# A two-layer graph network on one core: VectorE's maxima, shift, normalization and ELU results at other places of its order

## What is computed

```python
def _gat_layer(x, src, dst, W, a_src, a_dst, bias, concat):
    h = (x @ W).reshape(N, H, C)
    al_s, al_d = einsum('nhc,hc->nh', h, a_src), einsum('nhc,hc->nh', h, a_dst)
    e = leaky_relu(al_s[src] + al_d[dst], 0.2)
    m = segment_max(e, dst)
    ex = exp(e - m[dst])
    alpha = ex / (segment_sum(ex, dst)[dst] + 1e-16)
    out = segment_sum(h[src] * alpha[:, :, None], dst)   # concat or mean over heads, + bias

h = maximum(layernorm(x), 0)
x = x + gat_layer(elu(gat_layer(h, ..., 4 heads)), ..., 1 head)   # with self-loops
h = maximum(layernorm(x), 0)
x = x + gcn(relu(gcn(h)))       # D^-1/2 (A + I) D^-1/2 h W + b, twice
```

## Time and profile before

| what | value |
|---|---|
| median of 3 runs | 1179.64 us (1179.39 to 1180.54) |
| the profiled execution | 1182.3 us |
| its span | 1180.2 us |
| TensorE busy | 1115.9 us, 95% |
| VectorE busy | 839.0 us, 71% |
| ScalarE busy | 513.9 us, 44% |
| mean granted TensorE clock | 0.984 of full speed |
| first layer's rounds | about 245 to 750 us |
| second attention layer | about 780 to 905 us |

### The profile page before, as it was taken

One profiled execution on the slowest core, in us unless ns is written; L12 is line 12 of the kernel. 1 busy time (PEld: TensorE's weight loads), 2 busy tenths in 40 slices (PEclk: granted clock), 3 DMA queues, 4 the chain that ended last, 5 costly groups with the idle time before them and its releaser, 6 DMA issues. The chain is left out here.

```text
span 1180.2 us, 17595 instructions
## 1 busy us (share of the span) xinstructions
PE 1115.9 (95%) x7126; PEld 1045.3 (89%) x7126; DVE 839.0 (71%) x1394; ACT 513.9 (44%) x1052; POOL 54.3 (5%) x50
## 2 busy tenths in 40 slices
PE   5999999999999999999999999858999899999998
PEld 5878886789989998999999999758999899899998
DVE  7998896889768887789668778879757633341163
ACT  4232322376447654556547644335536612431110
POOL 4200001020000000000000000520000000000000
PEclk9999999989999999999999999968999999999999
DMA  6133130021011100201020100022002200000321
GB/s 230 68 103 117 41 122 18 1 63 54 1 42 49 54 1 1 90 22 34 1 68 23 54 1 1 10 91 72 27 27 103 83 1 1 27 14 1 131 77 55
DMA packets 27618, 58.44 MB, mean 50 GB/s; under 512 B 3492, under 2 KB 6152, under 8 KB 27536
## 3 DMA queue, kind: packets, MB, share of 16 engines
q1 hardware_dynamic: 27344, 56.96, 14.5%
q10 hardware_dynamic: 192, 0.32, 0.1%
HBM read 41.73 MB, written 15.54 MB: 49 GB/s over the span
## 5 line engine op out<-in xcount | busy, mean ns | idle before, releaser
L1456 PE MATMUL banks<-hs,ring_hi 128*128 128x258 f32 (+1 forms) x1600 | 299.8, 288 | 6.8 <-DVE z L1051 6.8
L1456 PEld LDWEIGHTS banks<-hs,ring_hi 128*128 128x128 f32 (+1 forms) x1600 | 249.0, 188 | 8.7 <-DVE z L1051 8.0
L1456 PE MATMUL banks<-hs,ring_lo 128*128 128x258 f32 (+1 forms) x800 | 227.1, 284 | 0.0
L247 ACT ACTIVATE e<-banks,al 128x256 f32<-128x256 f32 (+1 forms) x500 | 194.6, 493 | 38.0 <-PE banks L232 38.0
L1456 PEld LDWEIGHTS banks<-hs,ring_lo 128*128 128x128 f32 (+1 forms) x800 | 150.8, 189 | 0.0
L255 ACT ACTIVATE ring_hi<-pf 128x512 fp32r<-128x512 f32 (+1 forms) x125 | 81.6, 652 | 134.7 <-DVE pf L266 130.1
L1486 PE MATMUL banks<-w_hi,oT_hi 128*128 128x384 f32 (+1 forms) x320 | 109.5, 342 | 5.9 <-DVE shiftT L1130 4.5
L1486 PE MATMUL banks<-w_lo,oT_hi 128*128 128x384 f32 (+1 forms) x320 | 108.3, 338 | 0.0
L1486 PE MATMUL banks<-w_hi,oT_lo 128*128 128x384 f32 (+1 forms) x320 | 108.2, 338 | 0.0
L264 DVE TENSOR_TENSOR e<-e 128x512 f32<-128x512 f32 (+1 forms) x125 | 84.5, 676 | 33.2 <-ACT e L247 32.7
L1330 PE MATMUL banks<-w_hi,xT_hi 128*128 128x512 f32 x240 | 96.7, 403 | 1.2 <-DVE xT_lo L827 0.6
(11 more groups left out here) (265 smaller groups left out, 2106.2 us busy)
## 6 DMA issues: line engine op xcount, KB each, us to landing
h_scratch<-stage SPq DMA_DIRECT2D x30, 256.0 KB, 2.0
hs<-h_scratch SPq DMA_DIRECT2D x30, 256.0 KB, 2.9
w_st<-in_L_gnn_W SPq DMA_DIRECT2D x4, 1536.0 KB, 7.4
w_st<-in_L_gnn_W SPq DMA_DIRECT2D x16, 384.0 KB, 3.4
gw_st<-in_L_gnn_W SPq DMA_DIRECT2D x12, 384.0 KB, 4.2
xr<-in_x SPq DMA_DIRECT2D x9, 384.0 KB, 10.1
rows<-in_x SPq DMA_DIRECT2D x9, 384.0 KB, 5.8
x_scratch<-rows SPq DMA_DIRECT2D x9, 384.0 KB
```

The source lines that it names most:

```text
L247: last = nc.scalar.activation(self.e[:, local % 2, a, i, 0:n], self.p_shift[:, a, 0:n], ACT.Exp, bias=scores[a][:, g * G + i:g * G + i + 1])
L1456: last = nc.tensor.matmul(p_a[0:m, dt, half, 0:HH], wt.ring[a][:, s // G, s % G, dt * P:dt * P + m], hs[:, s, b, half * HH:(half + 1) * HH ...
```

## The change

No instruction is added or removed; instructions of VectorE and a few of TensorE stand at other places. With the diff's own order:

- In rounds c = 0 of heads 1 to 3, `normalize` of the last round and the first `add_products` block stand ahead of group 3's weights instead of behind them and group 2's low part.
- In rounds c = 4 of heads 0 to 2, `take_peaks(h, 0)` stands right behind the weights of group 0 and `take_peaks(h, 1)` right behind those of group 1 (they stood behind the low parts in groups 1 and 2). On TensorE the last two transposes of the maximum stand behind step 4 instead of 7, and the turned shift behind step 7 instead of 9. `keep_shift` stays in group 3.
- In every round `elu_out` stands ahead of group 4's weights (and in rounds c = 1 ahead of the split of weight parts 0 and 1), instead of between the low parts of groups 3 and 4.
- In the second layer the shift is turned behind step 4 and spread behind step 5 of chunk 0 (5 and 6 before), and in chunk 1 both `finish` calls stand behind group 2 instead of behind group 3.

```diff
--- before.py
+++ after.py
@@ -1135,7 +1135,12 @@
                     q = h * NC + c
                     last, second_last = before(q, 1), before(q, 2)
                     for g in range(NG - 1):
+                        if g == NG - 2 and c == 0 and h >= 1:
+                            normalize(last)
+                            add_products(second_last, range(1))
                         wt.weigh(nc, dve, counts, q, c, g)
+                        if c == NC - 1 and not final and g <= 1:
+                            take_peaks(h, g)
                         if second_last is not None and g == 0:
                             elu_lo(second_last, 0)
                         if q == 0 and g == 0:
@@ -1154,14 +1159,17 @@
                             nc.vector.tensor_copy(deg[:, :], p_d).then_inc(deg_done, 1)
                         if c == 0 and 1 <= g <= 2:
                             split_rows(h, g - 1)
-                        if c == NC - 1 and not final and g >= 1:
-                            (lambda: take_peaks(h, 0), lambda: take_peaks(h, 1), lambda: keep_shift(h))[g - 1]()
+                        if c == NC - 1 and not final and g == NG - 2:
+                            keep_shift(h)
                     scoring = final and c >= 2
                     row = (c - 2) * NDT
-                    if last is not None:
-                        normalize(last)
-                    if second_last is not None:
-                        add_products(second_last, range(2))
+                    if c == 0 and h >= 1:
+                        add_products(second_last, range(1, 2))
+                    else:
+                        if last is not None:
+                            normalize(last)
+                        if second_last is not None:
+                            add_products(second_last, range(2))
                     if c == 0:
                         split_rows(h, 2)
                     if not final:
@@ -1178,12 +1186,12 @@
                         add_products(second_last, range(3, NB))
                     if c == 0:
                         split_rows(h, 3)
+                    if last is not None:
+                        elu_out(last)
                     if c == 1:
                         split_weights(h, range(2))
                     wt.weigh(nc, dve, counts, q, c, NG - 1)
                     wt.lo(nc, dve, q, c, NG - 2)
-                    if last is not None:
-                        elu_out(last)
                     wt.lo(nc, dve, q, c, NG - 1)
                     if c == 0:
                         split_rows(h, NG - 1)
@@ -1420,12 +1428,12 @@
                     for t in range(8):
                         last = nc.tensor.transpose(p_g[t // 4][:, t % 4 * P:(t % 4 + 1) * P], top[:, t * P:(t + 1) * P], ident[:, :])
                     last.then_inc(top_t, 1)
-                if s == 7:
+                if s == 4:
                     pe.wait_ge(reduced, 3 * h + 3)
                     for t in range(8, T):
                         last = nc.tensor.transpose(p_g[0][:, (t - 8) * P:(t - 7) * P], top[:, t * P:(t + 1) * P], ident[:, :])
                     last.then_inc(top_t, 1)
-                if s == 9:
+                if s == 7:
                     turn_shift(h + 1, p_g[1][0:4 * T, 0:P])
 
             def turn_out(q, dt):
@@ -1518,7 +1526,7 @@
                 pe.wait_ge(shift_out, HEADS + 2)
                 wt.broadcast(nc, pe, pick, shiftT[:, 2, :], SECOND + 1, 1)
 
-            half.tensor(pe, {1: turn_rest, 5: lambda: turn_shift(HEADS + 1, p_shift_rest), 6: spread_rest})
+            half.tensor(pe, {1: turn_rest, 4: lambda: turn_shift(HEADS + 1, p_shift_rest), 5: spread_rest})
 
 
 BANDS = [(0, 3 * P), (3 * P, 3 * P), (6 * P, N - 6 * P)]
@@ -1847,12 +1855,14 @@
         dve.wait_ge(b_in, 16)
         residual(0)
         for c in range(1, NC):
+            ends = NG - 3 if c == 1 else NG - 2
             for g in range(NG - 1):
                 wt.weigh(nc, dve, counts, SECOND + c, c, g)
                 if g >= 1:
                     wt.lo(nc, dve, SECOND + c, c, g - 1)
-            for t in range((c - 1) * NDT, c * NDT):
-                finish(t)
+                if g == ends:
+                    for t in range((c - 1) * NDT, c * NDT):
+                        finish(t)
             wt.weigh(nc, dve, counts, SECOND + c, c, NG - 1)
             wt.lo(nc, dve, SECOND + c, c, NG - 2)
             wt.lo(nc, dve, SECOND + c, c, NG - 1)
```

## The result

The changed kernel takes **1172.36 us** (median of 7 runs, 1171.01 to 1175.7) where the kernel before took 1179.64 beside it on the same chip; the ratio is 0.9945, 95% interval 0.9926 to 0.9964. It is faster by about 7 us. The forecast was 1168.3 in a range of 1164.5 to 1173.3: the direction and the range held, the time near the range's upper end, and the gain of 11.3 us was too high by some 4. The profiled execution took 1172.36 us as well; its span is 1170.3, 9.9 less than the 1180.2 of the earlier trace rows. One execution of the experiment with the second layer's part alone took 1514.74 us at a mean granted clock of 0.677 and is left out of its ratio.

The account below looks back on a forecast made before the run. TensorE is busy nearly all of 1180.2 us, so only its waits or clock move the time. Terms -5.4 - 4.05 - 4.8 + 1.1 + 0.4 + 1.5 = -11.3 from 1179.64 give 1168.3 us, range 1164.5 to 1173.3.

Parts of the forecast that it names:

- The maxima and the shift: Round 4 of heads 0 to 2: maxima wait goes, 0.83 of the copy's wait stays; gain 1.81 us a head, 5.4 in three.
- The normalization: Rounds 5, 10 and 15: TensorE's wait for it goes; gain 1.35 us a head, 4.05 in three.
- The ELU results, rounds 6, 11 and 16: First transpose's gain goes into the second's wait for the turned low part; 0.14 us lost in each, 0.4 in all.
- The ELU results, round 1: Early results push weight parts and their load, so the turned low part delays the second transpose: 1.1 us lost.
- The clock behind the round-1 wait: TensorE's clock falls behind the new 2.3 us wait in round 1: 1.5 us lost, bounds 0 and 2.8.
- The second layer's rows: Second layer, first tile's rows: TensorE resumes at 810.45 instead of 812.44, 0.7 of wait left; gain 2.0 us.
- The clock behind the second layer's rows: With the wait there shortened, TensorE's clock stays up behind it: 2.8 us more gain.
- The carry-over to the median: Profiled execution, 2.7 us above the median of the runs: the forecast gain of 11.3 was taken off the median, 1179.64.
- Those at 1171.1 and 1173.1 us: Rivals, second layer: only 2.0 gained as the clock falls behind another wait, or nothing as sums hold the rows; chance 0.13.
- the one at 1171.3: Rival: the clock falls also behind the 1.7 us waits of rounds 6 and 11, 2 x 1.5 us more; chance 0.15.
- The rival in which the change is slower: Weight-load chain longer in every head: 1.1 + 2.8 = 3.9 us a head lost, +1.3 to +5.7 (1185.3 us); chance 0.03.

Follow-up runs that it names:

- the second trace: The changed kernel run again unchanged, for a second look at its waits and clock: 1173.78 us, ratio 0.9932 to the kernel before.

## Why the prediction was right, and where it was off

- **The maxima and the shift** (1.81 a head): right in mechanism, the term was too large. It measured 1.50, and the wait left is 1.06, not 0.83. The step that failed is "the exponentials of group 3 ... nothing ahead of them is moved": TensorE's own transposes of the maxima are, and they push the second transpose by 0.25.
- **The normalization** (1.35 a head): right. No wait at rounds 5, 10 and 15. That the early ELU results save this gain, with 0.3 us of slack, was right as well; without them the wait is 1.80.
- **The ELU results, rounds 6, 11 and 16** (0.14 lost in each): the waits were right, 1.99 and 1.72 where 1.7 was forecast, the loss was not. The two full pieces came within 0.01 and 0.22 of the forecast because two errors cancel: with 1.50 for the maxima and 1.35 for the normalization they would be 2.85 shorter, and they are 3.03 and 3.24 shorter, so the early results gained 0.2 and 0.4 in rounds 6 and 11. With the ELU results alone the same pieces are 130.75 and 130.57 us, 0.1 and 0.2 under those before. In round 16 they lost 0.5 in the first trace, with a wait of 0.80 that I had not forecast, and nothing in the second, where that wait did not come; ScalarE's wait for the load of part 3 there was 0.79 and 0.24.
- **The ELU results, round 1** (1.1 lost): the mechanism was right, the term too small: 1.7 lost (1.9 in the second trace). I followed the push of the load of part 2 alone. Counted from the start of round 1's sums, ScalarE's copy of part 2 starts 1.21 and 1.07 later in the two traces, as forecast, but that of part 3 starts 1.69 and 1.93 later (9.99 us before, 11.68 and 11.92 now), and that is the whole loss. ScalarE waits for the load of part 3 0.86 and 1.24 us where it waited 0.38:

```profile
270.81 0.85 ACT L672 ACTIVATE w_hi<-w_st 128x768 fp32r<-128x768 f32 x1 [0.38 <-DMA w_st<-in_L_gnn_W]
```

  VectorE's push is 1.13 of that; why the load of part 3 comes another 0.6 and 0.8 later is open. And the wait of 2.3 that I gave was worked out with the clock low ahead of it; with the clock at 1.00 there it is 4.65, with the clock low 3.36.
- **The clock behind the round-1 wait** (1.5): it fell, for about 6 us and not 3. In the changed kernel 59.39 - (58.31 - 1.50) = 2.6 us; in the second trace 59.27, 2.5 us.
- **The second layer's rows** (2.0): right. The wait is 0.89 (0.7 expected). The piece got shorter by 2.9, of which 2.0 is the wait; the rest goes with the clock behind the wait of 3.97 at its start, which was low for less long in that execution (0.50, 0.50, 0.52 and 1.00 over the four stretches of 2 us behind it, where before it was 0.50, 0.50, 0.50 and 0.54). That 0.9 is luck and no gain of the change.
- **The clock behind the second layer's rows** (2.8): from one profiled execution to the other it came out, at 2.69. (I counted 36 matmuls in the 6.50 us where the earlier trace rows shows 38; with 38 the term is 3.0.) But I read 0.51 from one execution and took it as what the wait costs in all. In six traces the wait of 2.9 cost 2.7 twice, 1.6 twice and nothing twice, 1.4 on average; the two that pay in full are those of the kernel before.
- **The carry-over to the median** ("it lies 2.7 above the median of the runs, and the difference is carried over"): this is the step that failed. The profiled execution of the changed kernel lies at its median, that of the kernel before 2.7 above its own, and so 9.9 between the two became 7 between the medians. The likely reason is that the 2.7 was itself time at the low clock, of the kind that the change removes, and could not be removed from an execution that has it and from the median as well: both traces of the kernel before that pay in full have a mean clock of 0.984, and half of its executions have 0.988 or more. It is not shown, since only the profiled executions have traces.

Of the 4.0 us by which the forecast was off, 2.6 are this and 1.4 its miss from profile to profile: 2.0 in head 0 and 0.3 elsewhere, less the 0.9 of luck. Taking the luck from the measured 9.9 and pricing the fall at 1.4 and not 2.7 gives 7.7 us, an estimate from these traces, beside the 7.3 between the medians and the 6.5 of the ratio (4.2 to 8.7 by its interval).

None of the rivals came true as written. Those at 1171.1 and 1173.1 us are nearest in time with the one at 1171.3, but the second layer's clock did not fall and its rows were not held. The one at 1171.3, a fall behind the waits of rounds 6 and 11, did not come in the first trace and came by half in the second. The rival in which the change is slower was the right place to fear: the loss in round 1 is 1.7 and 2.6, above its 1.1 + 2.8 together, but in the heads behind it no such loss came, only the 0.5 of round 16. What decides whether the clock falls in a given execution is still open.

## What to carry to other kernels

An instruction moved forward on a full engine is paid for by what it is moved past: follow each one that it delays to its load and to the engine that stands waiting for that load, because the best edit may be to move those (here it was worth more than the change itself, and on the kernel before, without the change, only about 2.5 us). Two moves can each be worth nothing and together worth something, so try them in pairs before dropping one. When a term is a fall of the clock, take it from several executions before giving it a price, ask whether the next wait takes it back, and don't carry an execution's distance from the median over a term that explains that distance.
